# Cross-attention in a decoder layer: the low part of the context is computed at another place in GpSimd's step

## The reference

```python
x = _layernorm(x + attn(x))                  # 16 heads, rotary positions
x = _layernorm(x + xattn(x, ctx_1024))       # one head of 256 features
x = _layernorm(x + ffn(x))                   # shared expert + 2 of 16 experts
# xattn, per sequence:
q = x @ Wq.T + bq;  k = ctx @ Wk.T + bk;  v = ctx @ Wv.T + bv
out = softmax(q @ k.T / sqrt(256)) @ v
```

## Time and profile before

| what | us |
|---|---|
| median of 3 runs | 1009.02 (1007.74 to 1020.84) |
| the profiled execution, its time | 1014.87 |
| its span, first to last instruction | 1012.9 |
| PE busy, share of the span | 846.4 (84%) |
| POOL busy, share of the span | 403.7 (40%) |
| mean granted TensorE clock, share of full | 0.926 |

### The profile page before, as it was taken

The page is one execution under the profiler, slowest core; times in us unless marked ns, Lnnn a source line. Parts: engine busy times, 40 slices in busy tenths (PEclk is TensorE's granted clock), DMA queues, the critical chain, the costliest instruction groups (busy, mean ns, idle before and its releaser), DMA issues. The chain is left out here.

```text
span 1012.9 us, 19460 instructions
## 1 busy us (share of the span) xinstructions
PE 846.4 (84%) x6042; PEld 683.0 (67%) x6043; DVE 652.7 (64%) x1479; ACT 474.4 (47%) x1098; POOL 403.7 (40%) x421
## 2 busy tenths in 40 slices
PE   3678888887888876688888898789996999999993
PEld 2455555555555543578888887668886999988883
DVE  5367777776767740257777665676654777857776
ACT  1125665665655763145555544324532545533443
POOL 4333333343333100367766663027771000037773
PEclk8579999999989986789999888999998999999998
DMA  2887999998988833546664542145754555534543
GB/s 72 222 201 184 226 241 256 224 232 209 237 221 234 204 83 81 94 70 144 140 132 111 99 110 94 62 142 183 260 180 151 172 166 164 177 103 136 184 125 95
DMA packets 194421, 162.67 MB, mean 161 GB/s; under 512 B 82480, under 2 KB 179376, under 8 KB 191280
## 3 DMA queue, kind: packets, MB, share of 16 engines
q1 hardware_dynamic: 177712, 134.50, 52.1%
q0 software_dynamic: 6144, 16.79, 5.2%
q10 hardware_dynamic: 10496, 10.49, 3.5%
HBM read 81.91 MB, written 75.37 MB: 155 GB/s over the span
## 5 line engine op out<-in xcount | busy, mean ns | idle before, releaser
L598 DVE TENSOR_REDUCE neg_m<-ps_s 128x2 f32<-128x512 f32 x256 | 168.9, 687 | 39.0 <-PE ps_s L352 38.9
L488 ACT ACTIVATE probs<-ps_t 128x512 f32<-128x512 f32 x256 | 147.1, 598 | 81.1 <-PE ps_t L358 77.0
L352 PE MATMUL ps_s<-k_stack,q_stack 48*128 48x256 f32 x512 | 118.5, 335 | 53.8 <-DVE neg_m L598 42.0
L352 PEld LDWEIGHTS ps_s<-k_stack,q_stack 48*128 48x128 f32 x512 | 76.3, 195 | 109.4 <-DVE neg_m L598 56.8
L111 PE MATMUL ps_f<-w_cross,w_sgu 128*128 128x512 f32 x552 | 133.6, 391 | 0.6 <-issue 0.6
L2045 POOL DMA_INDIRECT w_gu<-expert_outputs,pos x64 | 64.8, 1012 | 152.8 <-DMA expert_outputs<-low 134.3
L358 PE MATMUL ps_t<-q_stack,k_stack 49*128 49x256 f32 x512 | 118.6, 335 | 2.7 <-ACT probs L488 2.7
L111 PEld LDWEIGHTS ps_f<-w_cross,w_sgu 128*128 128x128 f32 x552 | 100.8, 188 | 19.9 <-issue 0.7
L111 PE MATMUL ps_g<-w_qkv,x_hl 128*128 128x512 f32 (+1 forms) x384 | 91.8, 390 | 18.5 <-DVE w_qkv L524 11.3
L111 PEld LDWEIGHTS ps_g<-w_qkv,x_hl 128*128 128x128 f32 x384 | 66.9, 216 | 36.7 <-DVE w_qkv L524 11.0
L2034 POOL DMA_INDIRECT expert_rows<-x_all,pos x64 | 68.6, 1071 | 37.7 <-issue 19.2
(11 more groups left out here) (208 smaller groups left out, 1745.7 us busy)
## 6 DMA issues: line engine op xcount, KB each, us to landing
stacks<-q_hl SPq DMA_DIRECT2D x48, 256.0 KB, 2.8
stacks<-k_hl SPq DMA_DIRECT2D x48, 256.0 KB, 3.3
q_stack<-stacks SPq DMA_DIRECT2D x32, 384.0 KB, 6.1
k_stack<-stacks SPq DMA_DIRECT2D x32, 384.0 KB, 9.3
expert_rows<-no_rows ACTq DMA_DIRECT2D x16, 640.0 KB, 5.8
low<-expert_rows SPq DMA_DIRECT2D x79, 128.0 KB, 2.1
expert_outputs<-low SPq DMA_DIRECT2D x79, 128.0 KB, 1.8
heads_out<-o_sb SPq DMA_DIRECT2D x32, 256.0 KB, 9.9
```

The lines of the kernel that those rows point to most:

```text
L352: by_query = pe.matmul(ps_s[n % 2][:, k * N:(k + 1) * N], q[q_rows, slab, k * P:(k + 1) * P], kk[q_rows, slab, :], start=True, stop=True)
L488: act.activation(probs[:, n % RING], ps_t[n % 2].rearrange("p (t q) -> p t q", t=TT), ACT.Exp).then_inc(exp_done, 1)
L598: dve.tensor_reduce(neg_m[c][:, :, row], ps_s[n % 2].rearrange("p (t k) -> p t k", t=TT), AX.X, ALU.max, negate=True).then_inc(max_done, 1)
```

## The change

In GpSimd's step, the call of `context_lo` moves from in front of `row_products` to behind `with_value_bias`. No instruction is added or removed, the data are the same, and no semaphore gets another count. The instructions of PE, DVE, ACT and SP stand in the same order as before.

```diff
                     norm_root(0, s)
                     if s.static and s.n == 0:
                         pool.wait_ge(folded, FOLDS)
-                    context_lo(s)
                     row_products(i, s)
                     with_value_bias(i, s)
+                    context_lo(s)
```

## The result

The changed kernel takes 1028.87 us (median of 4 runs, 1026.92 to 1035.79) against 1008.38 for the kernel before, timed beside it: a ratio of 1.0238, with a 95% interval of 1.0161 to 1.0315. It is slower; whether by more than 2%, this interval leaves open. When both were timed once more, later, the ratio was 1.0293 (1.0203 to 1.0383). The forecast was 1036 us, in a range of 1019 to 1050. The ratio is one of means, and one run of the kernel before (1020.84 us), in a slower state of the chip, is left out of it.

The account below looks back on a forecast made before the run. A circle through PE and line 1241 bounds the step. Twelve steps at 15.1 us add 27.1, four save 3.5: +23.6 on the profiled 1014.87 gives 1038.5, or 1032.6 if the profile's excess lies elsewhere; 1036 taken, range 1019 to 1050.

Parts of the forecast that it names:

- Line 1241 freed: DVE's normalization of x1 runs without c_lo beside it: 0.80 us a pair instead of 1.67, in each of 16 steps.
- c_lo, the store and line 1195: SP's x2 store, queued behind the wait for c_lo, lands at 7.42 us after line 1241, making line 1195 3.3 us late.
- Which clock: PE, idle about 3 us ahead of S2, falls to 1.2 GHz: steps between 14.5 and 15.6 us, taken as 15.1.
- its sign: Among the marks of a right forecast: twelve steps of cross-attention, 3 to 14, of 14.5 to 15.6 us each.
- The landing: The x2 store's DMA time, kept at 2.8 us; a landing of 2.3 would give a 14.0 us circle at full clock.
- Steps 0, 1, 2 and 15: Cross-attention steps without the late store, where line 1241's freed 0.87 us counts in full: -3.5 us together.
- The one at full clock: Rival: S2 always at 2.4 GHz, steps of 14.49 us, 1025 to 1031 us; 1 in 4, quicker landing included.
- The circle through the store: Step loop through POOL, SP and the DMA instead of PE: 7.45 + 6.24 + 0.80 = 14.49 us at full clock.
- The dear one: Rival: every S2 at half clock, 15.6 us steps, 1044 us, or line 1241 not freed, 1045; 3 in 20.
- The faster one: Rival: the x2 store stays hidden from line 1195, only the gain remains, 13.9 us off or more, 990 to 1001; 1 in 20.

Follow-up runs that it names:

- e4: The kernel before, with one more wait on POOL, for x1_done, ahead of the low part and the row products: 998.05 us, ratio 0.9958.
- e1: The changed kernel, with SP's load of the context moved behind the stores of x2 and of its transposes: 998.73 us, ratio to before 0.9932.
- e3: The changed kernel, with two tiles for x2 in turn and the wait for x2_out moved from DVE to ScalarE: 999.01 us, ratio 0.9905.

## Why the prediction was right, step by step

*Line 1241 freed: right.* 0.73 us a pair against the 0.80 forecast, and e4 shows that c_lo beside it was the cause. The Trainium skill (SBUF — State Buffer, Who interferes with whom) says that the two engines share a port pair, which the first comer holds for its whole instruction. The trace agrees on the order: a half takes 404 to 415 ns alone against 1347 to 1356 with c_lo 58 to 64 ns ahead of it. The long half ends 0.15 us after c_lo, though, sooner than the 0.41 that a half started at c_lo's end would take; no run shows the port itself.

*c_lo, the store and line 1195: right to a tenth.* c_lo ends at 3.81 (3.85 forecast), the store issues at 4.58 (4.62), line 1195 starts at 7.25 to 7.55 in the undisturbed steps (7.45), released by the store in all but one of the twelve. The six steps at a granted clock of 1.00 average 14.37 us (14.49 forecast). e1 and e3 each take this one wait away, by different means, and the loss is gone.

*Which clock: the mis-sized term.* The prediction took 15.1 us a step, midway between 14.49 at full clock and 15.6 with S2 at half clock, since PE would pause 3 us ahead of S2 in every step and fall to 1.2 GHz after it. The twelve steps average 14.75, and 14.53 without step 14, so the clock added about 0.16 us a step to the 14.37 and not 0.6. The pause is shorter than forecast: 1.93 us in the timeline, between 0 and 2.5 in steps 3 to 13, and 4.25 in step 14. PE's products end later than I had counted, 0.61 us of it a wait for the exponentials: AT ends 8.23 us after x1_done, not 7.41, and S2 starts at 10.17, not 10.46. And S2 ran at a lower clock in three steps only (2.74 us in step 3, 2.34 in step 10, 2.90 in step 14); in the others it took 1.66 to 1.69. Steps 8 and 10 show that the length of the pause doesn't decide this alone:

```profile
527.00 1.68 PE L111 MATMUL ps_x<-c_hl,xq_hl 128*128 128x256 f32 x12 [2.49 <-DVE xq_hl L1207]
...
555.52 2.34 PE L111 MATMUL ps_x<-c_hl,xq_hl 128*128 128x256 f32 x12 [2.36 <-DVE xq_hl L1207]
```

Six steps of twelve had a lower mean clock, and only some of these were longer (15.22, 14.95 and 14.75 against 14.29 and 14.47, besides step 14). So eight steps were shorter than the 14.5 to 15.6 us that the prediction named as its sign, and one was longer. Of the 7 us between 1036 and 1028.87, 12 x 0.35 = 4.2 are this term, net of step 14's late landing; the rest can't be assigned, since the median of the kernel before alone lay between 1003.93 and 1009.02 us from one set of runs to the next.

*The landing.* The median stayed 2.8 us. That a lighter load shortens it, which the Trainium skill (DMA: Bandwidth & Descriptors, Latency and other measured facts) led me to weigh, isn't seen: the step's DMA traffic fell from 132 to 110 GB/s and the median didn't move. The page's sentence is about HBM, and this store goes from one SBUF tile to another (x2 to x2_all), so it gave no reason for a shorter landing here. That it grows to 4.6 in step 14 I had no term for; it made line 1195 about 2 us later there.

*Steps 0, 1, 2 and 15: half right.* Steps 1 and 2 took 11.65 and 11.19 us against 12.95 and 12.12, a gain of 2.2 (1.7 forecast). Step 15 took 15.12 in one profile, at a mean clock of 0.86, and 12.25 in the other, at 1.00, against 13.61 at 0.88 before: the clock moved it more than the 0.87.

*The rivals.* The one at full clock (1025 to 1031, 1 in 4) came nearer than the forecast: 1028.87 lies inside it, six steps ran as it said, and without step 14 the average (14.53) is close to its 14.49. The circle through the store, which both share, put the time into the range; the half-way clock didn't. The dear one fell: S2 ran at a lower clock in three steps and line 1241 was freed. The faster one fell: the slack was 1.0 us, as its own condition said. Its price was wrong too. With the wait taken away (e1, e3), the gain by the ratios is about 7 and 10 us and not 14 to 25: of 0.94 us freed a step only about 0.15 remain at full clock, for the exponentials were next. Twelve steps at 0.15 and the 2.2 of steps 1 and 2 are 4 us; what the rest of the 7 and 10 is was not tried.

## What to carry to other kernels

Before a step is moved down in its queue, follow every semaphore it raises to the queue that waits there, and count what stands behind that wait: here a load needed two steps later held a store whose landing was due in 4 us. The slack of such a hidden wait (1.0 us) is read from the timeline, and what the move adds past it (3.3 us) comes on the step one to one, here less the 0.94 that it freed (12.04 to 14.37 us at full clock). Where a late producer can't be avoided, put the DMA that waits for it last in its queue, or give the tile behind it a second buffer; either alone undid the loss here.

## What I had not expected of the hardware

Pauses of PE of 1.1 to 2.5 us ahead of S2 left the granted clock at 1.00 in six of twelve steps, where in the earlier trace rows a stretch with 1.3 us of idle time was followed by 0.50. And in both profiles of the changed kernel one step waited longer for its store (line 1195 at 9.36 and 8.70 us after x1_done, not 7.4), with landings of 4.6 and 3.9 us for 256 KB in place of 2.8. Over the ten profiles, every landing of 3.9 us or more of a cT load or an x2 store went with a 16 KB instruction packet that began while the transfer was under way.
